# A graph network on one core: the flush of the second and third gather layers in pairs of tiles, and VectorE's adds in two instructions instead of four

## The reference

```python
# layer 0: attention scores by source and edge type, tails summed by source
aggr = segment_sum(sigmoid(concat(x[src], rel[type]) @ att_w + att_b) * x[dst], src)
x = layernorm(x + tanh(aggr @ W_w.T + W_b))
# layer 1: sum by destination, the node's own row where it has no edge
agg = segment_sum(x[src], dst);  deg = segment_sum(1, dst)
x = layernorm(x + where(deg > 0, agg, x) @ W.T + b)
# layer 2 and layer 3: weighted sums by destination
x = layernorm(x + segment_sum(x[src] * edge_weight, dst))
x = layernorm(x + segment_sum(x[src] * edge_weight * edge_weight_n2, dst))
```

## Time and profile before

| | |
|---|---|
| median of 3 runs | 11881.73 us (11879.01 to 11899.44) |
| profiled execution | 11878.79 us, span 11877.0 us |
| granted TensorE clock, mean | 0.806 |
| PE busy | 8897.3 us (75%), 49605 instructions |
| DVE busy | 7726.7 us (65%), 19171 |
| ACT busy | 5860.3 us (49%), 13187 |
| POOL busy | 8022.3 us (68%), 7169 |

### The profile page before, as it was taken

The page is one execution under the profiler, slowest core; times in us unless marked ns, Lnnn a source line. Parts: engine busy times, 40 slices in busy tenths (PEclk is TensorE's granted clock), DMA queues, the critical chain, the costliest instruction groups (busy, mean ns, idle before and its releaser), DMA issues. The chain is left out here.

```text
span 11877.0 us, 171360 instructions
## 1 busy us (share of the span) xinstructions
PE 8897.3 (75%) x49605; PEld 5666.5 (48%) x49606; DVE 7726.7 (65%) x19171; ACT 5860.3 (49%) x13187; POOL 8022.3 (68%) x7169
## 2 busy tenths in 40 slices
PE   4787888888886455566666787888887788888887
PEld 2444444444444234444546455454445455554445
DVE  8777777777774655544444776666665776666665
ACT  4766555555553444333332665544443766544443
POOL 5787788888887566666665566666665566666665
PEclk8877777777776676767777899989988899889998
DMA  5433333334334211111111111111111111111111
GB/s 145 47 38 35 36 37 38 39 38 38 38 38 70 51 25 25 25 25 24 24 24 27 27 24 25 25 25 24 25 24 28 28 25 25 25 25 25 23 24 30
DMA packets 651932, 398.90 MB, mean 34 GB/s; under 512 B 456994, under 2 KB 563748, under 8 KB 649745
## 3 DMA queue, kind: packets, MB, share of 16 engines
q0 software_dynamic: 445920, 252.47, 17.5%
q1 hardware_dynamic: 201276, 132.08, 4.3%
q10 hardware_dynamic: 3814, 3.37, 0.1%
HBM read 283.23 MB, written 104.16 MB: 33 GB/s over the span
## 5 line engine op out<-in xcount | busy, mean ns | idle before, releaser
L801 POOL DMA_INDIRECT mem<-xt,mem x5175 | 4910.8, 949 | 2864.1 <-issue 1338.3
L1148 PE MATMUL ps<-mem 128*128 128x392 f32 (+5 forms) x6750 | 2905.2, 536 | 1079.8 <-DVE mem L1708 448.9
L722 POOL DMA_INDIRECT table<-mem,idx x1925 | 3000.4, 1559 | 746.4 <-issue 556.7
L1708 DVE TENSOR_TENSOR mem<-mem,ps 128x392 f32 (+3 forms) x3300 | 1917.4, 581 | 1966.8 <-remote 1007.5
L943 ACT ACTIVATE mem<-iota_f,mem 128x128 f32<-128x128 f32 x4200 | 1319.3, 390 | 2659.8 <-remote 1312.7
L1160 PE MATMUL ps<-mem,xs 128*64 128x94 f32 (+1 forms) x17640 | 2068.5, 271 | 382.5 <-issue 363.2
L1160 PEld LDWEIGHTS ps<-mem,xs 128*64 128x64 f32 (+1 forms) x17640 | 1803.8, 156 | 1026.7 <-issue 979.8
L1689 DVE TENSOR_SCALAR mem<-ps,mem 128x392 f32<-128x392 int16 (+5 forms) x4050 | 2175.9, 556 | 0.0
L1148 PEld LDWEIGHTS ps<-mem 128*128 128x128 f32 (+1 forms) x6750 | 1106.1, 184 | 1936.5 <-issue 1312.5
L922 ACT COPY mem<-zero_c 128x658 f32<-128x658 f32 x1260 | 895.6, 732 | 1370.5 <-remote 896.1
L1181 PE MATMUL ps<-mem 128*64 128x64 f32 (+1 forms) x10350 | 1031.7, 245 | 478.4 <-issue 456.2
(11 more groups left out here) (180 smaller groups left out, 7819.2 us busy)
## 6 DMA issues: line engine op xcount, KB each, us to landing
mem<-xt,mem POOLq DMA_INDIRECT x5175
mem<-key_rows SPq DMA_DIRECT2D x385, 160.0 KB
table<-mem,idx POOLq DMA_INDIRECT x1925
table<-mem POOLq DMA_DIRECT2D x3, 6304.0 KB
mem<-table SPq DMA_DIRECT2D x42, 448.0 KB, 5.2
xt<-xs SPq DMA_DIRECT2D x9, 896.0 KB
mem<-in_x_dram SPq DMA_DIRECT2D x415, 16.0 KB
w_d<-mem SPq DMA_DIRECT2D x2, 1562.5 KB, 7.8
```

Of the source, the lines that this page charges most:

```text
L722: pool.indirect_dma_start(out=tables[i % NTAB][:, :], out_offset=bass.IndirectOffsetOnAxis(ap=idx[:, i % (IDXS * GC):i % (IDXS * GC) + 1], ...
L801: pool.indirect_dma_start(out=gbuf[:, o:o + F], out_offset=None, in_=xt[l][:, :], in_offset=bass.IndirectOffsetOnAxis(ap=src_q[q % 2].bitc ...
L1148: last = pe.matmul(ps_d[b % PSD][:, 0:w], lo_l[:, r * P:(r + 1) * P], blk_l[:, r * DT:r * DT + w], start=(k == 0), stop=(k == parts - 1))
L1708: v.tensor_tensor(at, at, new, ALU.add).then_inc(d_add[l], 1)
```

## The change

For l = 1 and 2, `flush_zone` takes two tiles at once: weights of 128 columns (64 of each tile), moving operand of 188 columns (94 of each). Of the 128 x 188 result the two diagonal blocks are the sums that are wanted, and `flush_add` adds them into the lower and the upper half of `acc` (two TENSOR_TENSORs). `acc` now holds a part of each sum in partitions 64 to 127; `sums_out` folds both together by a matmul with `fold`, two identities on top of each other. For this `xs` is packed to 64 columns a tile after layer 1 (`x_of`), and POOL clears all 128 partitions of `acc`. The 14 zones have 6 and 8 tiles in turn, in all layers (for l = 0 still tile by tile).

In all gather layers `Row` loads the values without the move for each, and in `block_add`, `tail_add` and `flush_add` the wait is attached to the TENSOR_TENSOR. A wait that another one implies is left out in `tail_add`.

```diff
-ZONES = [(z * T // FZ, (z + 1) * T // FZ) for z in range(FZ)]
+ZONES = [(2 * (z * (T // 2) // FZ), 2 * ((z + 1) * (T // 2) // FZ)) for z in range(FZ)]
...
+        fold = sb("fold", [P, F])
...
-        ps_f = ps[:, 6 * BK:6 * BK + WC]
+        ps_f = ps[:, 6 * BK:6 * BK + 2 * WC]
...
-                self.r = [eng.alloc_register(f"{nm}{k}") for k in range(8)]
+                self.values = ()
 
             def value(self, i):
                 if i % 8 == 0:
-                    self.eng.load(self.r, self.row[:, i:i + 8])
-                return self.eng.snap(self.r[i % 8], min_val=0, max_val=self.most)
+                    self.values = ()
+                    _, self.values = nc.values_load_multi_w_load_instructions(
+                        self.row[:, i:i + 8], engines=[self.eng.engine], min_val=0, max_val=self.most,
+                        skip_runtime_bounds_check_because="the row is clamped to these bounds where it is made",
+                        bass_reorder=False)
+                return self.values[i % 8]
...
+        x_of = [x3[:, :, 0:F]] + [xs[:, 0:T * F].rearrange("p (j f) -> p j f", f=F)] * 3
...
-                pool.memset(acc[0:F + 1, lo * BN:hi * BN], 0.0).then_inc(acc_zero, 1)
+                pool.memset(acc[:, lo * BN:hi * BN], 0.0).then_inc(acc_zero, 1)
...
-                    for t in range(*ZONES[z]):
-                        last = pe.matmul(ps_f[0:M, :], xs[:, t * XW:t * XW + M],
-                                         dense[s_ % 2][:, t * WC:(t + 1) * WC], start=(t == 0),
-                                         stop=(t == T - 1), skip_group_check=True)
+                    if l == 0:
+                        for t in range(*ZONES[z]):
+                            last = pe.matmul(ps_f[0:M, 0:WC], xs[:, t * XW:t * XW + M],
+                                             dense[s_ % 2][:, t * WC:(t + 1) * WC], start=(t == 0),
+                                             stop=(t == T - 1), skip_group_check=True)
+                    else:
+                        for t in range(*ZONES[z], 2):
+                            last = pe.matmul(ps_f, xs[:, t * F:(t + 2) * F], dense[s_ % 2][:, t * WC:(t + 2) * WC], start=(t == 0),
+                                             stop=(t == T - 2), skip_group_check=True)
...
-                        at = acc[0:F, (b * BT_ + k) * P:(b * BT_ + k + 1) * P]
-                        last = pe.transpose(ps_O[b % 2][:, k * F:(k + 1) * F], at, ident[0:F, 0:F])
+                        at = acc[:, (b * BT_ + k) * P:(b * BT_ + k + 1) * P]
+                        last = pe.matmul(ps_O[b % 2][:, k * F:(k + 1) * F], at, fold[:, :], start=True, stop=True)
...
+            v.tensor_tensor(fold[:, :], ident[:, 0:F], ident[:, F:P], ALU.add)
...
-                    if b:
-                        v.wait_ge(d_add[l], b)
                     v.wait_ge(blk_sum[l], b + 1)
...
-                    v.tensor_tensor(at, at, new, ALU.add).then_inc(d_add[l], 1)
+                    ins = v.tensor_tensor(at, at, new, ALU.add)
+                    if b:
+                        ins._wait_ge(d_add[l], b)
+                    ins.then_inc(d_add[l], 1)
 
                 def flush_add(s_, added, l=l, M=M):
-                    at = acc[0:M, ds(bases.value(s_), WC)]
-                    v.wait_ge(acc_add[l], added)
+                    base = bases.value(s_)
+                    at = acc[0:M, ds(base, WC)]
                     v.wait_ge(flush_done[l], (s_ + 1) * FZ)
-                    v.tensor_tensor(at, at, ps_f[0:M, :], ALU.add).then_inc(f_add[l], 1)
+                    if l:
+                        up = acc[F:2 * F, ds(base, WC)]
+                        v.tensor_tensor(up, up, ps_f[F:2 * F, WC:2 * WC], ALU.add)
+                    v.tensor_tensor(at, at, ps_f[0:M, 0:WC], ALU.add)._wait_ge(acc_add[l], added).then_inc(f_add[l], 1)
 
                 def tail_add(n, flushed, l=l, M=M):
                     at = acc[0:M, ds(cols.value(n), WD)]
-                    if n:
-                        v.wait_ge(acc_add[l], n)
-                    if flushed:
+                    if n and flushed > ZONE_END[max(n - 1, 0)] // FZ:
                         v.wait_ge(f_add[l], flushed)
                     v.wait_ge(agg_done[l], n + 1)
-                    v.tensor_tensor(at, at, ps_w[n % 2][0:M, :], ALU.add).then_inc(acc_add[l], 1)
+                    ins = v.tensor_tensor(at, at, ps_w[n % 2][0:M, :], ALU.add)
+                    if n:
+                        ins._wait_ge(acc_add[l], n)
+                    ins.then_inc(acc_add[l], 1)
```

More of the change, by code:

```diff
@@ L612, in store @@
                 sp.dma_start(to[lo * P:whole * P, :].rearrange("(j p) f -> p j f", p=P),
-                             x3[:, lo:whole, 0:F]).then_inc(x_out, 16)
+                             x_of[l][:, lo:whole, :]).then_inc(x_out, 16)
             for b in range(NB):
@@ L691, in _ @@
                     fixup(l)
-            sp.dma_start(out[(T - 1) * P:N, :], x3[0:LAST, T - 1, 0:F]).then_inc(x_out, 16)
+            sp.dma_start(out[(T - 1) * P:N, :], x_of[3][0:LAST, T - 1, :]).then_inc(x_out, 16)
             sp.wait_ge(x_out, (4 * len(SLICES) + 1) * 16)
@@ L1468, in _ @@
             yv = y[:, 0:T * F].rearrange("p (j f) -> p j f", f=F)
-            xv = x3[:, :, 0:F]
+            xv = x_of[0]
             keys0(0)
@@ L1585, in scales @@
                         link(v.reciprocal(rstd[:, lo:hi], var[:, lo:hi]))
-                        v.tensor_tensor(xv[:, lo:hi, :], yv[:, lo:hi, :], bc(rstd[:, lo:hi], hi - lo, F),
+                        v.tensor_tensor(x_of[k][:, lo:hi, :], yv[:, lo:hi, :], bc(rstd[:, lo:hi], hi - lo, F),
                                         ALU.mult).then_inc(x_new, 1)
@@ L1767, in plus_x @@
                     v.wait_ge(o_done[l], b + 1)
-                    v.tensor_tensor(batch(yv, b), ps_O[b % 2].rearrange("p (j f) -> p j f", f=F), batch(xv, b),
+                    v.tensor_tensor(batch(yv, b), ps_O[b % 2].rearrange("p (j f) -> p j f", f=F), batch(x_of[l], b),
                                     ALU.add).then_inc(o_used[l], 1)
```

## The result

The changed kernel takes 11793.25 us (median of 4 runs, 11784.05 to 11803.89) against 11882.83 us for the kernel before in the same comparison: a ratio of 0.9921, interval 0.9906 to 0.9936, 94 us by that ratio. The profiled execution took 11793.26 us with a span of 11791.6, 85.4 less than before. Forecast were 11863 and faster: the sign and the range hold, the size does not.

A forecast was written before the change was run, and what follows sets the result against it. The prediction took gather bursts plus TensorE's late count, 7.35 us a slot, as the bound. Layers 2 and 3 -30, layer 1 0, ends +11, together -19: 11860, or 11863 on the median's scale; range 11740 to 11905.

The forecast's parts named there:

- The lock: Gather layers: five gathers of 6.25 us, then 1.1 us until TensorE's late count, 7.35 us a slot whatever TensorE does.
- mid layer there is almost nothing above the lock: Layers 2 and 3: 204 gathers per 300 us in both windows, so the flush's relief of TensorE mostly becomes idle time.
- the 8 a layer: Layers 2 and 3: gain from the flush in pairs, of at most about 55 and 34 us open.
- The start's 7: First 46 slots of layers 2 and 3: shorter waits of DVE's adds save about 7 us a layer.
- layer 1, "nothing": Layer 1: the shorter adds of DVE were forecast to gain 0 us.
- Its own signs: Checks in the trace: gathers per window, flush records, zone times, end stage; wrong if layers shorten over 30, layer 1 moves over 10.
- its 202 to 205: Windows of 300 us in layer 2: the count of gathers expected to stay; 210 or more would refute the lock.
- TensorE's relief: Flush of layers 2 and 3: fewer records and less issue idle free 0 to 139 us a layer, about 63 taken.
- The ends: End stages of layers 2 and 3: 14 matmul records replace seven transposes, TensorE sets the pace, +5.5 us a layer, +11 in all.
- The lock loosens: Rival: with half the flush instructions counts land earlier, POOL stands less; about -130 with the ends, 11750; chance 0.28.
- Zones of eight: Rival: eight-tile zones take 1.43 us against 1.28 and delay the blocks behind; +42, 11924; chance 0.15.
- The pairs give nothing: Rival: the 128-wide load isn't hidden and eats the switches; layers stay, ends cost 11, 11893; chance 0.07.

The follow-up runs named there:

- short flush: The changed kernel with one pair per zone in layers 2 and 3, the sums of the other pairs left out: 11733.4 us, ratio 0.9873.
- adds alone: The kernel before with the new Row and two-instruction adds, flush still tile by tile in zones of seven: ratio 0.9963, 44 us faster.
- pairs alone: The changed kernel with the old Row and the old four-instruction adds of VectorE: ratio 0.9973, 32 us faster than the kernel before.

## Why the prediction was right in sign and wrong in size

- **The lock** is real: a short flush changed the layers by 35 and 26 us, leaving out the gathers by 640. But the prediction took it as a fixed 7.35 us a slot. It is a price per gather (1.25 and 0.17 us) and about 0.3 per stop, and where POOL goes through into the next five it pays one stop for two slots. The row that tells it was in the prediction's hands: the 2.45 us of the earlier trace rows, called the same pair as 1.40, is a stop behind ten gathers.
- **The failed step** is "mid layer there is almost nothing above the lock" and the 8 a layer taken from it: mid layer gave all of the 40. The start's 7 didn't come: by slot 46 layers 2 and 3 had gained 2.4 and 0.9 us. So -15 a layer was -40, and layer 1, "nothing", was -13. The count of 204 gathers in both layers hid the room, since layer 1 was not at the floor either: adds alone took 11 us and 25 stops out of it. In layer 2 78 stops fewer give some 23 us at 0.3 each, and the stops that are left are shorter by the rest of 39.
- **Its own signs** said so: a layer shorter by more than 30 us, or layer 1 moved by more than 10, was to make the forecast wrong, and both came. The 206 and 207 gathers lie above its 202 to 205 and below the 210 that would have spoken against the lock.
- **TensorE's relief** was taken at 63 us a layer, and it was more. Of the 0.17 us a zone that fewer records could give at most, the prediction took 0.07, and 0.16 came, 67 us in place of 29; the idle time of "issue" before the flush fell by 25, where 34 were taken. The wide load is hidden: its records last 0.19 us in the trace, and the products follow one another every 0.16. The forecast zones of 1.1 and 1.4 us are met only by the timeline's 1.12 and 1.44, which count the modelled end of the last record; from start to start, as the 1.28 was read, they are 0.96 and 1.28. The fixed 2.5 ns a matmul of the Trainium skill ("TensorE: Matmul & The Clock Gate", section "Wait — 56ns, not 53.3ns?") would be 0.02 us of a zone, so the trace gives far more than the rule; what else the records of 94 columns cost is not shown.
- **The ends** were right: +5.5 forecast (its own working, 45 less 40, gives 5), +6.0 and +6.1 measured, by the mechanism named (2.99 us of TensorE above 2.38, clock 0.50).
- **The rivals.** "The lock loosens" was given -130 with layers 2 and 3 shortened by some 66 each, layer 1 by 10. Measured -40 and -13: it came a good half of the way, and the range held because it had been drawn down to this rival's value. "Zones of eight" costs 19 us alone, tile by tile; in pairs its 1.43 us is 1.28, and its ground is gone in layers 2 and 3. "The pairs give nothing" is refuted by pairs alone, 32 us (20 to 45).

## What to carry to other kernels

When two layers with different loads show the same pace, the pace is set outside of them, but equality does not say that it is a floor: leave out the suspected setter and see how far the time falls, as the layer without gathers did. Relief of an engine that is not the bound can still pay through the number of stops of the engine that is, so count stops, not only their time. When two kernels are laid beside each other by windows, let the windows begin at the same event, and read a zone from start to start. An f32 matmul that replaces a transpose doubles the records, and at a clock of 0.50 each took 0.21 us in place of 0.11; a few products ahead of the stage brought that back for six of 14 batches.

## What the runs showed of the hardware

Counts of TensorE reach VectorE and POOL late, and TensorE itself idles for "issue" before the flush, only while indirect gathers run: mid-layer slots of 7.3 us fell to 5.1 with no gather, and idle time of the flush from 52 to 2 us. The gathers' own rate was 1.45 to 1.47 us each in bursts at 1.25, at 62% and at 81% TensorE load with five a slot, at 71% and 90% with four. The mean clock of TensorE fell with its load: 0.772 over the kernel with the short flush, 0.797 with the whole, and the former was the faster. And a TensorE without idle time is no sign of the full clock: in the last stage the trace shows none for 42.07 us, at 0.50.
